# Cross attention of the first stage: scores computed once, scaled probabilities turned by TensorE, output projection once per batch

## The reference

```
q = (xq @ wq).reshape(b, sq, H, DH).transpose(0, 2, 1, 3)
k = (ctx @ wk).reshape(b, sk, H, DH).transpose(0, 2, 1, 3)
v = (ctx @ wv).reshape(b, sk, H, DH).transpose(0, 2, 1, 3)
scores = jnp.einsum('bhqd,bhkd->bhqk', q, k) / math.sqrt(DH)
attn = jax.nn.softmax(scores, axis=-1)
out = jnp.einsum('bhqk,bhkd->bhqd', attn, v)
out = out.transpose(0, 2, 1, 3).reshape(b, sq, INNER)
return out @ wo + bo
```

## Time and profile before

| | before |
|---|---|
| median of 3 runs (lowest to highest) | 2491.66 us (2486.72 to 2500.01) |
| the profiled execution | 2493.45 us, of which the span is 2491.9 us |
| mean granted TensorE clock | 0.925 of full speed |
| PE busy | 2136.4 us (86%) |
| DVE busy | 1625.6 us (65%) |
| ACT busy | 1158.8 us (47%) |
| POOL busy | 158.0 us (6%) |

### The profile page before, as it was taken

The page is one execution under the profiler, slowest core; times in us unless marked ns, Lnnn a source line. Parts: engine busy times, 40 slices in busy tenths (PEclk is TensorE's granted clock), DMA queues, the critical chain, the costliest instruction groups (busy, mean ns, idle before and its releaser), DMA issues.

```text
span 2491.9 us, 32453 instructions
## 1 busy us (share of the span) xinstructions
PE 2136.4 (86%) x11272; PEld 942.0 (38%) x11272; DVE 1625.6 (65%) x3877; ACT 1158.8 (47%) x2209; POOL 158.0 (6%) x165
## 2 busy tenths in 40 slices
PE   7999898899989988878887887888788788868898
PEld 4555433555556642233232223222332322232433
DVE  6767477566655787666746775685577467753564
ACT  4555232134333335635663665566366646634311
POOL 0000000021112010000000000000000000010000
PEclk9999988899999998989997999798899979978999
DMA  4000000300001100000100100010000000030000
GB/s 152 1 1 1 1 1 1 120 1 1 1 1 54 28 20 26 2 26 4 42 1 26 45 1 23 5 44 1 26 24 22 1 26 27 1 106 1 0 1 9
DMA packets 38034, 54.35 MB, mean 22 GB/s; under 512 B 5073, under 2 KB 34546, under 8 KB 36338
## 3 DMA queue, kind: packets, MB, share of 16 engines
q1 hardware_dynamic: 37874, 52.28, 6.7%
HBM read 32.34 MB, written 0.52 MB: 13 GB/s over the span
## 4 chain that ended last, share of the span: by engine, by line
PE 40%; DVE 10%; ACT 8%; issue 4%; SPq 1%; DMA 0%; ACTq 0%; DVEq 0%
PE ps L2022 7%; PE ps L2002 5%; ACT big L2502 4%; PE ps L1983 4%; DVE C_nm L2679 4%; PE ps L2067 3%; PE ps L2150 3%; PE ps L2257 2%; PE ps L2162 2%; PE ps L2253 2%; ACT big L2582 2%; PE ps L2278 2%; PE ps L2169 2%; PE ps L2178 2%; PE ps L2127 1%
## 5 line engine op out<-in xcount | busy, mean ns | idle before, releaser
L2679 DVE TENSOR_REDUCE C_nm<-ps 128x1 f32<-128x512 f32 x768 | 501.6, 686 | 181.5 <-PE ps L1983 177.2
L2502 ACT ACTIVATE big<-ps 128x512 f32<-128x512 f32 x768 | 427.8, 596 | 232.4 <-PE ps L2002 222.3
L1983 PE MATMUL ps<-C_attn 62*128 62x512 bf16 x768 | 276.8, 417 | 60.0 <-DVE C_nm L2679 51.1
L2002 PE MATMUL ps<-C_attn 64*128 64x512 bf16 x768 | 253.2, 397 | 62.9 <-ACT big L2502 52.1
L2022 PE MATMUL ps<-big,C_attn 128*32 128x512 f32 x1536 | 213.5, 629 | 13.3 <-ACT big L2502 13.3
L1983 PEld LDWEIGHTS ps<-C_attn 62*128 62x128 bf16 x768 | 63.5, 94 | 300.3 <-DVE C_nm L2679 166.0
L2002 PEld LDWEIGHTS ps<-C_attn 64*128 64x128 bf16 x768 | 59.2, 93 | 277.0 <-ACT big L2502 203.7
L2582 ACT ACTIVATE big<-ps,C_biasx 77x512 f32<-77x512 f32 x192 | 115.5, 678 | 55.6 <-PE ps L2154 55.4
L2641 ACT ACTIVATE big<-ps 128x512 f32<-128x512 f32 (+1 forms) x66 | 39.4, 597 | 152.0 <-PE ps L2253 149.7
L3000 DVE TENSOR_TENSOR big<-big,ps 128x512 f32<-128x512 f32 x64 | 44.0, 688 | 94.1 <-PE ps L2257 74.2
L2773 DVE TENSOR_REDUCE C_nmx<-ps 128x4 f32<-128x308 f32 x192 | 77.9, 472 | 40.1 <-PE ps L2131 39.9
(11 more groups left out here) (385 smaller groups left out, 3696.6 us busy)
## 6 DMA issues: line engine op xcount, KB each, us to landing
C_attn<-C_first SPq DMA_DIRECT2D x144, 128.0 KB, 2.4
C_w<-in_C_w SPq DMA_DIRECT2D x6, 1090.0 KB, 5.2
C_attn<-in_D_ew SPq DMA_DIRECT2D x4, 1536.0 KB, 10.4
big<-in_B_ew SPq DMA_DIRECT2D x8, 514.0 KB
normw_later<-in_norm_w SPq DMA_DIRECT2D x1, 2304.0 KB, 16.0
A_w<-in_A_w SPq DMA_DIRECT2D x2, 1024.0 KB, 11.6
A_w<-in_A_w SPq DMA_DIRECT2D x2, 768.0 KB, 8.6
B_w<-in_B_w SPq DMA_DIRECT2D x1, 1536.0 KB, 10.9
```

What stands on the lines that cost most here:

```text
L1983: pe.matmul(ps[:, bank, :], lhsT=qs[side(hp, MAX_ROW), b, 2 * q + pq, t * P:(t + 1) * P], rhs=ks[side(hp, MAX_ROW), b, 2 * q + pq, :], sta ...
L2002: pe.matmul(ps[:, bank, :], lhsT=ks[side(1 - hp, HALF), b, 2 * q + pq, kt * P:(kt + 1) * P], rhs=qs[side(1 - hp, HALF), b, 2 * q + pq, :], ...
L2502: act.activation(prob[:, kt % 2, pq, 1 - hp, :], ps[:, bank, :], ACT.Exp, scale=SCALE)\
L2679: dve.tensor_reduce(nm[:, q % 2, t, pq, hp:hp + 1], ps[:, bank, :], AX.X, ALU.max, negate=True).then_inc(emptied[bank], 1)
```

## The change

Scores are computed once, with the tokens on partitions. DVE takes the row maxima and writes the scores less the maximum to SBUF (128 x 616: two heads, four token tiles, 77 keys). ACT takes the exponential there, in place; the factor 0.125 goes to the copy of the queries. DVE sums the rows and inverts the 128 x 8 sums, and POOL multiplies the probabilities by them. PE turns them in eight f32 transposes to 77 x 128 each, ACT copies the turned bank pair (77 x 1024), PE weighs, and DVE copies the weighted values out. The output projection waits until a batch's eight pairs are there: 32 f32 matmuls of 128 x 128 for batch 0 at u = 11, and for batch 1 after the loop, 24 for the first six pairs and 4 for each of the last two. It comes out with the tokens on partitions and is added to y at once. The loop runs two passes longer, the unit that is turned lies two behind the scores, and the one that is weighed three.

```diff
-    S_BANK, ST_BANK, PV_BANK, DEN_BANK, OUT_BANK, MISC = 0, 2, 4, 5, 6, 7
-    CONSTS = 4
+    S_BANK, T_BANK, PV_BANK, MISC = 0, 4, 6, 7
+    HEAD_AT, OUT_AT = 3, PAIRS + 3
     half = lambda h: slice(DH * h, DH * (h + 1))
+    pair = lambda n: S_BANK + 2 * (n % 2)
...
+            nc.sbuf_tensor(name + "_p", [P, 3, 2, TB, CTX], F32) as prob, \
+            nc.sbuf_tensor(name + "_pT", [CTX, 2, 2, S], F32) as pT, \
+            nc.sbuf_tensor(name + "_cn", [P, PAIRS, S], F32) as cn, nc.Block() as block:
+
+        along = lambda x: x.rearrange("p h (t o) -> p h t o", o=1).broadcast_to([P, 2, TB, CTX])
+        score = lambda n: ps[:, pair(n):pair(n) + 2, 0:TB * CTX].rearrange("p h (t k) -> p h t k", k=CTX)
...
+            for n in range(N):
+                pool.wait_ge(inverted, n + 1)
+                one = prob[:, n % 3, :, :, :]
+                pool.tensor_tensor(one, one, along(rden[:, n % 2, :, :]), ALU.mult).then_inc(scaled, 1)
...
-                elif n == 1:
-                    pe.wait_ge(q_ready, 1)
                 else:
-                    pe.wait_ge(nmT_ready, n - 1)
+                    pe.wait_ge(q_ready, n)
...
+                if n >= 2:
+                    pe.wait_ge(shifted, n - 1)
...
+            def turn(n):
+                pe.wait_ge(scaled, n + 1)
                 if n:
-                    pe.wait_ge(exp_done, n)
+                    pe.wait_ge(pT_ready, n)
                 for h in range(2):
-                    pe.matmul(ps[0:CTX, ST_BANK + h, :], lhsT=kT[half(h), p, b, :], rhs=qT[half(h), n % 3, :],
-                              start=True, stop=False)
-                for h in range(2):
-                    last = pe.matmul(ps[0:CTX, ST_BANK + h, :], lhsT=ones2[half(h), :], rhs=nmT[half(h), n % 2, :],
-                                     start=False, stop=True)
-                last.then_inc(st_done, 1)
+                    for t in range(TB):
+                        last = pe.transpose(ps[0:CTX, T_BANK + h, t * P:(t + 1) * P], prob[:, n % 3, h, t, :], m.ident[:])
+                last.then_inc(turned, 1)
...
             def weigh(n):
                 b, p = divmod(n, PAIRS)
-                pe.wait_ge(exp_done, n + 1)
+                pe.wait_ge(pT_ready, n + 1)
                 if n:
                     pe.wait_ge(cn_ready, n)
                 for h in range(2):
-                    last = pe.matmul(ps[half(h), DEN_BANK, :], lhsT=ones[0:CTX, :], rhs=prob[:, n % 2, h, :],
-                                     start=True, stop=True)
-                last.then_inc(den_done, 1)
-                for h in range(2):
-                    last = pe.matmul(ps[half(h), PV_BANK, :], lhsT=v[:, b, p, half(h)], rhs=prob[:, n % 2, h, :],
+                    last = pe.matmul(ps[half(h), PV_BANK, :], lhsT=v[:, b, p, half(h)], rhs=pT[:, n % 2, h, :],
                                      start=True, stop=True)
                 last.then_inc(pv_done, 1)
...
+            def project_out(t, pairs, out):
+                for p in pairs:
+                    last = pe.matmul(out, lhsT=cn[:, p, t * P:(t + 1) * P], rhs=w[:, p, WO:WO + P],
+                                     start=p == 0, stop=p == PAIRS - 1)
+                return last
...
+            for u in range(N + 2):
+                late = u in (HEAD_AT, OUT_AT)
+                if u == HEAD_AT:
+                    pe.wait_ge(q_ready, u + 1)
+                    head.turn(pe, ps[:, MISC, :]).then_inc(head.turned, 1)
+                if u == OUT_AT:
+                    pe.wait_ge(q_ready, u + 1)
+                    pe.wait_ge(cn_ready, PAIRS)
+                    for t in range(TB):
+                        last = project_out(t, range(PAIRS), ps[:, MISC, t * P:(t + 1) * P])
+                    last.then_inc(out_done, 1)
+                if u + 1 < N and not late:
+                    queries(u + 1)
+                if u == N:
+                    pe.wait_ge(q_ready, N)
+                    tail.turn(pe, ps[:, MISC, :]).then_inc(tail.turned, 1)
                 if u >= 2:
+                    turn(u - 2)
+                if u < N:
+                    scores(u)
+                if u >= 3:
+                    weigh(u - 3)
+                if u == HEAD_AT:
+                    pe.wait_ge(head.hT_ready, 1)
+                if u == OUT_AT:
+                    pe.wait_ge(y_added, 1)
+                if late:
+                    queries(u + 1)
+            pe.wait_ge(shifted, N)
+            for t in range(TB):
+                project_out(t, range(PAIRS - 2), ps[:, t, 0:P])
             weigh(N - 1)
+            pe.wait_ge(cn_ready, N - 1)
+            for t in range(TB):
+                project_out(t, (PAIRS - 2,), ps[:, t, 0:P])
+            pe.wait_ge(cn_ready, N)
+            for t in range(TB):
+                last = project_out(t, (PAIRS - 1,), ps[:, t, 0:P])
+            last.then_inc(out_done, 1)
...
+                act.activation(qT[:, n % 2, :], ps[:, MISC, :], ACT.Copy, scale=SCALE).then_inc(q_ready, 1)
             def exps(n):
+                act.wait_ge(shifted, n + 1)
+                one = prob[:, n % 3, :, :, :].rearrange("p h t k -> p (h t k)")
+                act.activation(one, one, ACT.Exp).then_inc(exp_done, 1)
+
+            def copy_turned(n):
+                act.wait_ge(turned, n + 1)
                 if n >= 2:
                     act.wait_ge(pv_done, n - 1)
+                act.activation(pT[:, n % 2, :, :], ps[0:CTX, T_BANK:T_BANK + 2, :], ACT.Copy).then_inc(pT_ready, 1)
...
+            for u in range(N + 2):
+                late = u in (HEAD_AT, OUT_AT)
+                if u == HEAD_AT:
                     act.wait_ge(head.turned, 1)
+                    head.copy(act, ps[:, MISC, :]).then_inc(head.hT_ready, 1)
+                if u + 1 < N and not late:
+                    copy_q(u + 1)
+                if u == N:
+                    act.wait_ge(tail.turned, 1)
+                    tail.copy(act, ps[:, MISC, :]).then_inc(tail.hT_ready, 1)
+                if u >= 2:
+                    copy_turned(u - 2)
+                if late:
+                    copy_q(u + 1)
+                if u < N:
+                    exps(u)
...
+            def shift(n):
                 dve.wait_ge(s_done, n + 1)
+                c.after(dve.tensor_reduce(most[:], score(n), AX.X, ALU.max))
+                if n >= 3:
+                    dve.wait_ge(turned, n - 2)
+                dve.tensor_tensor(prob[:, n % 3, :, :, :], score(n), along(most[:]), ALU.subtract).then_inc(shifted, 1)
+            def invert(n):
+                dve.wait_ge(exp_done, n + 1)
+                c.after(dve.tensor_reduce(sums[:], prob[:, n % 3, :, :, :], AX.X, ALU.add))
+                if n >= 2:
+                    dve.wait_ge(scaled, n - 1)
+                dve.reciprocal(rden[:, n % 2, :, :], sums[:]).then_inc(inverted, 1)
+            def take(n):
                 dve.wait_ge(pv_done, n + 1)
+                if n == PAIRS:
+                    dve.wait_ge(out_done, 1)
+                dve.tensor_copy(cn[:, n % PAIRS, :], ps[:, PV_BANK, :]).then_inc(cn_ready, 1)
+            def add_out(b, source):
+                dve.wait_ge(out_done, b + 1)
                 y = m.y[:, b * TB:(b + 1) * TB, :]
+                dve.tensor_tensor(y, y, source, ALU.add).then_inc(y_added, 1)
+                dve.wait_ge(y_added, b + 1)
...
+            for u in range(N + 2):
+                if 1 <= u <= N:
+                    invert(u - 1)
+                if u == OUT_AT:
+                    add_out(0, ps[:, MISC, :].rearrange("p (t d) -> p t d", t=TB))
+                if u < N:
+                    shift(u)
+                if u >= 3:
+                    take(u - 3)
                 if u < 2:
                     head.root(dve, 2 * u)
                     head.root(dve, 2 * u + 1)
                 if u == 1:
                     head.apply(dve)
+                if u == OUT_AT:
                     tail.begin(dve)
                     tail.stats(dve)
+                if u in (OUT_AT + 1, OUT_AT + 2):
+                    tail.root(dve, 2 * (u - OUT_AT - 1))
+                    tail.root(dve, 2 * (u - OUT_AT - 1) + 1)
+                if u == OUT_AT + 3:
                     tail.apply(dve)
+            take(N - 1)
+            add_out(1, ps[:, 0:TB, 0:P])
...
-            for t in range(TB):
-                last = pe.transpose(m.ps[:, 6, t * P:(t + 1) * P], out[:, t * P:(t + 1) * P], m.ident[:])
-            last.then_inc(o_turned, 1)
...
-            dve.wait_ge(o_turned, 1)
-            y = m.y[:, TB:2 * TB, :]
-            dve.tensor_tensor(y, y, m.ps[:, 6, :].rearrange("p (t d) -> p t d", t=TB), ALU.add).then_inc(out_added, 1)
-            dve.wait_ge(out_added, 1)
```

## The result

The changed kernel takes 2460.18 us in the median of 4 runs (2449.97 to 2462.91), against 2494.55 us of the kernel before in the same comparison: ratio 0.9857, 95% interval 0.9816 to 0.9898. That is 34.4 us, 1.4%, clear of the 0.5% bound of the prediction. The profiled execution took 2462.91 us, of which the span is 2461.3.

The account below looks back on a forecast made before the run. PE was taken to set the 6.135 us unit, with the clock low for a third of the stage. A 42 us gain less 11 for the clock gave 31, so 2461 us; 8-in-10 range 2446 to 2481.

Parts of the forecast that it names:

- the 0.5% bound of the prediction: Whole kernel: about 12.5 us is what a measurement tells from no change; below 2479 counts as faster.
- The unit: Middle units at the upper clock level: PE's unit falls from 6.135 to 3.88 us, with the chain hidden beside it.
- rival C: POOL's product in each unit takes 3 us: units of 4.3, a gain of 25, 2467 us; chance 0.08.
- The upper-level schedule: Whole stage timed step by step at clock 1.00, waits included: feed-forward starts at 392.7 against 434.93, gain 42 us.
- the sum without the clock: Stage schedule with PE always at the upper level: feed-forward starts at 392.7 against 434.93, gain 42 us.
- The fall in the fill: While the pipe fills, PE's waits of 1 to 4 us drop the clock to its lower level for 20 us.
- The spell forecast for the tail: End of the stage: PE's waits of 5.2, then 2 us bring another 8 to 10 us at the lower level.
- the term of 11 us: Loss to the lower clock in fill and tail: 28 x 0.48 = 13 us, of which some 2 fall into waits.
- Rivals A and B: A: clock low from about 310 to the projection, gain 8, 2484, chance 0.10; B: to stage's end, 15 slower, 2507, 0.05.
- The shared access: SBUF port shared by POOL and DVE: norm steps beside POOL's products could lose 4.5 us at most; taken as 0.
- Rival D: Behind the stage the gain is given back, as the second stage waits for something late anyway: no change, 2491; chance 0.03.

Follow-up runs that it names:

- the two doublings: Changed kernel with each unit's eight transposes done twice: stage 105.4 us, unit 4.86; changed kernel with POOL's product done twice: stage 104.75 us, units 4.20.

## Why the prediction was right, point by point

- **The size.** 2461 was forecast and 2460.18 measured; 2462.4 on the profiled execution against 2462.91. The range held. That it came this close is partly luck: the runs spread over 13 us, and the gain on the medians is 34.4 where 31 was forecast, mostly since the kernel before came out 2.9 us slower in this comparison.
- **The unit.** 3.88 was worked out, 3.99 measured: L943 and L963 take 1.05 and 1.01 from start to start in their new neighbourhood, not 0.95 and 0.96. The transposes' 0.97 was right (0.96), and the queries take 0.97, not 1.00. That PE binds, not the chain, is shown by the two doublings. POOL took 1.22, so rival C had no ground.
- **The upper-level schedule.** turn(0) came at 309.1 (308.8 forecast), turn(1) at 314.7 (314.2). The wait ahead of the projection was 1.41 us instead of 2.5. From scores(4) on all comes 7 to 9 us later than in the sum without the clock: the end came at 401.8, where that sum gave 392.7, and 404 with the clock.
- **The clock.** The fall in the fill came as forecast, ahead of it the 2.42 us wait, but lasted 13.7 instead of 20 us. The spell forecast for the tail did not come: PE's waits there were 1.27 and 1.21 us, not the 5.2 and 2 taken, since the last transposes and weighings stand in them. One of 3.4 us came inside the projection instead (9.0 against 7.5 us). Of the 9.1 us by which the end came later than the sum without the clock, some 1.2 are the unit's 0.11 us, so the term of 11 us, worked out from 28 us at the lower level where there were 17, was nearer 8. Rivals A and B did not happen: the clock rose again among units a quarter of which is transposes. The Trainium skill (TensorE: Matmul & The Clock Gate, Part 4: PE-mode transpose) says that transposes do not count as busy in the way matmuls do; the run with twice as many, at 1.00 throughout, shows that 1.84 us of them in a unit of 4.86 us did not bring the clock down here. Whether a transpose counts for less than a matmul no run measures, for none has a stretch of transposes alone.
- **Where the gain comes from.** Here the working was thinner than its sum. It said of the inversion that it costs nothing in the middle units, which holds (36.81 us with and without it), gave it no term at the ends, and gave PE's shorter unit the credit. The runs say otherwise. The shorter inversion alone makes the stage 20.2 us shorter, of which 15.7 at the ends of the batches, half by waits and half by the clock, are its own; the 4.5 in the fill are a shorter low spell that it cannot have caused. With the clock at 1.00 on both sides, the rest of the change is worth 109.46 - 94.55 = 14.9 us. And in the changed kernel PE's shorter unit needs the shorter inversion: with it put back, the stage is slower than before. The sum came out because it was made as a schedule with all waits in it and set against the measured end of before, 434.93, in which the inversion's waits and low spells stand, though no term names them. A unit's saving times sixteen, (6.135 - 3.88) x 16 = 36 us, would have left them out.
- **The shared access** was rightly taken as nothing, and for the reason given, the order, but by a margin of only 0.1 us: in the run with the product twice two norm steps were caught, for 1.05 and 0.45 us.
- **Rival D** did not happen: the second stage starts 34.4 us earlier, and of that 30.5 is left at the end of the profiled execution, in which the stages behind it spend some 10 us more at the lower level.

## What to carry to other kernels

An operation that hides in the steady state can still cost much at the ends of a loop, where nothing covers it, and by the clock falls that stand at its waits: price it there too (15.7 us here, where the whole change shortens the stage by 33.4). When a change shortens the binding engine's unit, first ask whether the next engine's unit is shorter than the new one; here DVE's had to shrink first. Where PE waits a microsecond or two while a pipe fills, idle matmuls into a free bank can cost less than the lower clock, and here work spread over the units was better than one late piece. When two kernels' stages differ by a few microseconds, compare where their low spells stand before a cause is named: one profile each cannot tell a cause from a spell that came out shorter.

## What was not expected of the hardware

- POOL's product with a factor repeated over 77 columns took 1.216 us for 616 columns, 1.97 ns a column, where a product of two full tiles took 1.268 us for 512, 2.48 ns a column.
- Doubling the transposes, 14 us of PE more, lengthened the stage by 3.4 us only, since the clock then did not fall. What this leaves open is the cause: whether the first transposes' longer run, the shorter wait behind it (1.99 instead of 2.42 us) or chance kept it up wasn't told apart.
- Behind the same rows of PE the lower level lasted 13.7 us in one kernel and 23.9 in another, and behind the same wait of 3.24 us 3.4 and 10.2 us.
